# All five scatter transfers of an expert, not the fourth and fifth alone, wait for the next expert's second products

## The reference, cut to what matters

```python
x = x + attention(layernorm(x))                     # 16 heads of 8, window of 64
xf = layernorm(x).reshape(4096, 128)
shared = silu(xf @ sg) * (xf @ su) @ sd
top_idx, gates = top-4 of 32 experts per token      # 4 of 8 groups first
buf[e, pos] = xf[token]                             # 640 places per expert
h = silu(buf[e] @ wg[e]) * (buf[e] @ wu[e])         # 128 -> 256
out_e = h @ wd[e]                                   # 256 -> 128
routed[token] += gate * out_e[e, pos]               # for each kept (token, k)
return x + shared + routed
```

## Time and profile before

| | |
|---|---|
| median of 3 runs | 623.31 us (621.44 to 626.21) |
| profiled execution, first to last instruction | 719.4 us; no other time of this execution is given |
| PE, PEld busy | 573.4 us (80%), 459.8 us (64%) |
| DVE, ACT, POOL busy | 418.4 us (58%), 322.5 us (45%), 350.9 us (49%) |
| mean granted TensorE clock | 0.891 |
| HBM | read 50.00 MB, written 54.30 MB |

### The profile page before, as it was taken

The page is one execution under the profiler, slowest core; times in us unless marked ns, Lnnn a source line. Parts: engine busy times, 40 slices in busy tenths (PEclk is TensorE's granted clock), DMA queues, the critical chain, the costliest instruction groups (busy, mean ns, idle before and its releaser), DMA issues.

```text
span 719.4 us, 20830 instructions
## 1 busy us (share of the span) xinstructions
PE 573.4 (80%) x7427; PEld 459.8 (64%) x7427; DVE 418.4 (58%) x1281; ACT 322.5 (45%) x832; POOL 350.9 (49%) x394
## 2 busy tenths in 40 slices
PE   4578988788778888675758798888888888798685
PEld 2346756556555556454535688888888888788553
DVE  5766778587777777553435555444445554454155
ACT  4255756455665655443433243334444433343310
POOL 8210143555555554555567045555555555655610
PEclk9579999899999999987679898999999999999998
DMA  7899888566666444300000233322334334332069
GB/s 249 235 242 241 246 229 259 152 204 199 175 188 192 133 113 106 73 18 18 9 10 8 73 117 122 96 85 83 114 99 119 116 112 129 119 104 77 17 246 343
DMA packets 79417, 98.33 MB, mean 137 GB/s; under 512 B 12097, under 2 KB 59999, under 8 KB 79216
## 3 DMA queue, kind: packets, MB, share of 16 engines
q1 hardware_dynamic: 65280, 82.92, 39.5%
q0 software_dynamic: 9216, 12.02, 5.4%
q10 hardware_dynamic: 4848, 2.40, 1.1%
HBM read 50.00 MB, written 54.30 MB: 145 GB/s over the span
## 4 chain that ended last, share of the span: by engine, by line
PE 35%; another core or an unknown queue 13%; issue 11%; ACT 11%; SPq 8%; DMA 7%; POOL 7%; DVE 5%; ACTq 1%; POOLq 1%; DVEq 0%
PE banks L1122 9%; PE banks L1148 7%; SPq L352 4%; ACT yout L812 4%; PE banks L939 3%; DMA rload<-pair_results 3%; DMA rotated_keys<-parts 3%; POOL expert_slots L491 3%; ACT hact L793 2%; SPq L393 2%; PE banks L889 2%; PE banks L920 2%; ACT pt L662 2%; DVE mx L1246 2%
## 5 line engine op out<-in xcount | busy, mean ns | idle before, releaser
L625 POOL DMA_INDIRECT pair_results<-yout,yidx x160 | 156.2, 976 | 135.0 <-ACT yout L812 91.8
L491 POOL DMA_INDIRECT expert_slots<-xfe,sidx x128 | 128.3, 1002 | 133.3 <-issue 51.9
L1122 PE MATMUL banks<-xgT_parts,wgu_parts 128*128 128x320 f32 x768 | 149.1, 347 | 29.2 <-ACT hact L793 29.2
L1122 PEld LDWEIGHTS banks<-xgT_parts,wgu_parts 128*128 128x128 f32 x768 | 126.9, 209 | 40.5 <-ACT hact L793 33.1
L1508 DVE TENSOR_TENSOR hact<-hact,banks 128x320 f32<-128x320 f32 x128 | 57.0, 482 | 130.5 <-ACT hact L793 119.3
L662 ACT ACTIVATE pt<-banks 128x512 f32<-128x512 f32 x128 | 69.5, 595 | 78.9 <-PE banks L920 53.3
L1246 DVE TENSOR_REDUCE mx<-banks 128x8 f32<-128x1024 f32 x64 | 78.2, 1222 | 45.2 <-PE banks L889 43.5
L812 ACT ACTIVATE yout<-banks,ypair 128x128 f32<-128x128 f32 x160 | 44.7, 372 | 122.8 <-remote 61.8
L1148 PE MATMUL banks<-wdn,hact 128*128 128x128 f32 x640 | 85.3, 293 | 2.7 <-DVE hact L1508 1.7
L1148 PEld LDWEIGHTS banks<-wdn,hact 128*128 128x128 f32 x640 | 85.1, 212 | 3.1 <-issue 3.1
L793 ACT ACTIVATE hact<-banks 128x320 f32<-128x320 f32 x128 | 53.4, 452 | 48.6 <-PE banks L1122 30.0
(11 more groups left out here) (155 smaller groups left out, 945.8 us busy)
## 6 DMA issues: line engine op xcount, KB each, us to landing
expert_slots<-xg SPq DMA_DIRECT2D x32, 325.0 KB, 4.7
xg<-expert_slots SPq DMA_DIRECT2D x32, 325.0 KB
pair_results<-zero SPq DMA_DIRECT2D x32, 256.0 KB
rload<-pair_results SPq DMA_DIRECT2D x16, 512.0 KB, 9.5
kS<-rotated_keys SPq DMA_DIRECT2D x32, 240.0 KB
qS<-rotated_queries SPq DMA_DIRECT2D x32, 192.0 KB
wgu<-in_L_ffn_wg_dram SPq DMA_DIRECT2D x32, 128.0 KB
wgu<-in_L_ffn_wu_dram SPq DMA_DIRECT2D x32, 128.0 KB
```

The costliest lines, as they stand in the source:

```text
L491: g.indirect_dma_start(out=slots_d, out_offset=bass.IndirectOffsetOnAxis(ap=sidx[:, m % NB, j, k:k + 1], axis=0), in_=xfe[:, m % NB, j, k, ...
L625: g.indirect_dma_start(out=pairs_d, out_offset=bass.IndirectOffsetOnAxis(ap=yidx[:, c, j:j + 1], axis=0), in_=yout[:, c, j, :], in_offset= ...
L1122: last = mm(bank[2 + 2 * w + h][:, 0:CH], wgu_parts[:, e.b, wp, w, h * P:(h + 1) * P], xgT_parts[:, e.b, xp, ch * CH:(ch + 1) * CH], start ...
```

## The change

The extra wait moves from the fourth transfer of an expert to its first. Since a queue runs in order, all five transfers now stand behind it. The last expert has no such wait, before and after. Nothing else differs: the same transfers, the same counts, the same buffers.

```diff
             def scatter(e, c, more):
                 pool.wait_ge(S.yidx_ready, e + 1)
                 for j in range(ST):
-                    if j == 3 and more:
-
-
+                    if j == 0 and more:
                         pool.wait_ge(S.h_mul, 4 * e + 8)
-
                     pool.wait_ge(S.y_evac, ST * e + (j + 1))
```

## The result

The changed kernel takes 638.3 us (median of 4 runs, 638.16 to 638.81) against 624.58 us of the kernel before (4 runs, 621.44 to 626.21): a ratio of 1.030, 95% interval 1.026 to 1.034. It is slower, by 13.7 us.

What follows compares the result with a forecast made beforehand. In the profile a ring of PE, ACT and POOL with the hold bounds the stage; timed runs were taken as free of it, near 6.3 us a step. 623.3 + 0 (fourth transfer) + 0 (stage) + 2.4 (end) = 625.7 us, range 617 to 646.

Steps and rivals of the forecast that it cites:

- the likeliest case: Whole kernel: time within one per cent, 6.2 us; the forecast (0.42) and Rival 4 (0.14) together, 0.56.
- Rival 1: VectorE's L1514 waits for the scatter two before, 15 us per microsecond 1.67 exceeds 1.64; 629 to 644 us, chance 0.12.
- The hold: Expert stage, profiled trace: PE's third product's signal appears only when the scatter has landed; 2.15 us a step, 67 us.
- rivals 2 and 3: 2: hold also in timed runs, 700 us, chance 0.20; 3: it hits only late signals, 617 to 560 us, 0.12.
- The fourth transfer's wait is met on arrival: zero: POOL's scatter before: second products end before the fourth transfer comes, so taking the wait from there changes 0 us.
- Each scatter starts 2.46 us later: POOL's first transfer: starts 0.90 us behind the second products, at 549.39 in place of 546.93.
- A shift is kept but not added up: POOL's queue: five transfers fill 6.38 us, no room at a 6.30 step, yet the delay does not grow.
- 1.67 against a cover of 1.64: VectorE's L1514 at a 6.30 step: waits 1.67 us for the landing, PE's first products have 1.64 spare; taken as zero.
- The end: 2.4 us: After the stage: expert 30's later scatter pushes expert 31's, its landing and SP's first load, adding 2.4 us.
- Rival 4: POOL's queue: transfers come late anyway, so the moved wait does nothing; 623 us, chance 0.14.
- ScalarE's cover: Evacuation L812, waiting for the scatter of two before: 6.0 us spare at step 8.45, 1.7 at 6.30; cost zero.
- Rival 3's lower price: Expert stage: the step falls by only a tenth of the 2.15 us, giving 617 us.

Runs made afterwards that it cites:

- experiment 1: The kernel before, unchanged, profiled a second time (the second profile of before): 624.31 us, span 622.2 us.
- experiment 4: The kernel before without the extra wait for the second products at all: 619.25 us, ratio 0.999.
- experiment 3: The kernel before with the wait moved to the first transfer for expert 30 alone: 622.22 us, ratio 0.999.
- 7 and 8: Four scatter transfers an expert instead of five, in the kernel before (611.2 us, ratio 0.980) and in the changed kernel (614.64 us, ratio 0.984).
- experiment 5: The kernel before with the extra wait at the second transfer in place of the fourth: 627.63 us, ratio 1.005.

## Why the prediction was right and where it failed

The range of 617 to 646 held 638.3, but the likeliest case (no change, 0.56) did not come, and the sum, 625.7, was 12.6 us short. Rival 1 came, which had 0.12 and a price of 629 to 644; the range holds the result because rival 1 was taken into it. Its sign, L1514 waiting for `pair_results` in most steps, tells little by itself: the wait occurs 24 times after, but 21 times in the second profile of before.

- **The hold.** It was read out of one execution, and experiment 1 shows that it is no property of the kernel. The bet that the timed runs don't have it was right; rivals 2 and 3 fall with it. A span 15% above the median was reason to doubt that profile more than I did: it hid the real state of the stage, in which POOL is as full as PE.
- **The fourth transfer's wait is met on arrival: zero.** Right, within what the runs can tell (experiment 4).
- **Each scatter starts 2.46 us later.** Wrong as stated. Where a first transfer waits in a step of the usual length, it starts 3.6 us behind the first evacuation, as 1.18 + 2.46 has it, and the 0.90 us behind the second products is right to the hundredth (521.84 to 522.74). But the queue of the kernel before is behind by itself: its scatters already start 1.2 to 3.9 us behind the first evacuation, so most are moved by less.
- **"A shift is kept but not added up" on POOL.** This failed too. It needs a single shift. Here a late landing makes the products late, late products hold POOL, and POOL's idle time can't be made up at 5 x 1.276 = 6.38 us of transfers to PE's 6.3 to 6.4. So the queue stays where its fifth transfer meets SP's load, and it happens again nearly every third step.
- **The step that failed: 1.67 against a cover of 1.64, taken as zero.** The mechanism, its place and its cover were right: where VectorE waits 1.67 us (508.97), PE stands 0.17. The term that was mis-sized is the landing, and not in every step but in about one of three. I took 1.2 us from the end of the last transfer to its landing, that is 2.2 from its start, and 21 of the first 30 landings of the changed kernel are within 0.5 us of it. In its chain of waits a late one and the last one, counted from the start of the transfer, are

```profile
513.42 3.61 DMA pair_results<-yout,yidx
...
603.25 2.12 DMA pair_results<-yout,yidx
```

2.12 at the quiet end, close to the 2.02 of the earlier trace rows, but 3.61 at 513.42, 1.5 us more. So VectorE waits 3.42 us there, not 1.67; less the cover of 1.64 that is 1.78 late, and PE stands 1.72. At 15 us for each microsecond beyond the cover the prediction's own price gives 27 us for the stage; 18.35 were measured. That the price came near is partly luck: it counted every second step, while nine of 31 were longer (eight of more than 8 us, one of 7.2), and some 3.4 us are the clock's. The Trainium skill (DMA: Bandwidth & Descriptors, Latency and other measured facts) has HBM accesses at 2 us under high load. The estimate drawn from it, 1.8 us later, is near the 1.5 us of the late landings, but no run shows that the load on HBM makes them late, and most landings in the same stage are not.
- **The end: 2.4 us.** Zero (experiment 3), because expert 30's wait is met when the queue gets there; 2.04 us once the queue isn't behind (7 and 8). Rival 4's point, a wait hidden by a queue that is late anyway, was right at this place.
- **ScalarE's cover** held. The view lists 11.8 us in 5 steps as ended by the landing, but these idle times are 2.3 to 2.5 us each, like those that PE's third product ends (2.32 to 2.39).
- **Rival 3's lower price** left out the end term: a tenth of 67 us below 625.7 is 619, not 617. Nothing hangs on it.

Why some landings take 3.3 us and more is not settled. All but one come together with SP's load (the last section has the counts), but no run moved the loads alone.

## What to carry to other kernels

A wait that is met on arrival at a late place in a queue need not be at an early one, and when the queue has as much work in a step as the engine that bounds the stage, what it loses is not made up. A shift can also cost in another way than by its own length, here by putting a queue's last transfer beside another queue's load. Look for who must wait for the end of that queue's work, and put that wait as late in the waiting engine's order as the need for its result allows: here moving three statements turned a loss of 3% into none, and gave 1% in the kernel before. And when one profile's span is far from the median, take a second one before building on its waits.

## What the runs showed of the hardware

A transfer of the scatter that starts while VectorE's L1533 runs (two inputs in SBUF) takes longer. In the second profile of before:

```profile
501.58 0.68 DVE L1533 TENSOR_TENSOR wgu_parts<-wgu,wgu_parts 128x512 fp32r<-128x512 f32 x1
501.73 1.37 POOL L625 DMA_INDIRECT pair_results<-yout,yidx  x1 [0.30 <-ACT yout L812]
```

1.37 us against a median of 0.97, for a start 0.15 us into L1533. In that profile all 14 transfers that start 0.04 to 0.30 us into an L1533 take 1.23 to 1.49 us, the longer the earlier they start, and no other transfer takes more than 1.00. The Trainium skill says of such instructions that they contend with GpSimd for SBUF (GPSIMD Engine Reference, Key points); the trace agrees, with 0.3 to 0.5 us. Over the stage it is small: 157.2 us of transfers after, 160.7 before.

A scatter's last transfer lands late when a load of rows is issued beside it. In the traces from experiment 1 on and that of the changed kernel, SP's load L331 was issued between 0.3 us before and 0.62 us after the start of the last transfer of 43 scatters (of the first 30 of each kernel), and all 43 landed 3.3 to 4.0 us after that start. Where the load came 0.8 us or more after it, or 1.9 us or more before, 243 scatters landed after 2.1 to 2.7 us. In between (0.62 to 0.8 us) 12 landed after 2.6 to 3.9 us. Of 32 with no such load within 3 us, one landed late (3.5 us, experiment 5, expert 28). That the load is the cause was not tested.
